# Norm ahead of the feed-forward stage: transposes and per-token statistics in place of averages over partitions, and the side work of the cycles dealt out anew

## What is computed

```python
def _layer(x, wqkv, qs, ksc, wo, lg, lb, w1, b1, w2, b2):
    q, k, v = split(shift_token(x) @ wqkv)        # 8 heads of 64
    q, k = rotary_xpos(l2norm(q) * qs, l2norm(k) * ksc)
    o = local_attention(q, k, v)                  # windows of 64, each looks one window back
    x = x + o @ wo
    h = shift_token(x)                            # features 64..127 come from the token before
    mu = h.mean(-1, keepdims=True)
    var = h.var(-1, keepdims=True)
    h = (h - mu) / jnp.sqrt(var + 1e-05) * lg + lb
    h = h @ w1 + b1
    a, g = jnp.split(h, 2, axis=-1)
    return x + (a * gelu(g)) @ w2 + b2
```

## Time and profile before

| | |
|---|---|
| device time, median of 3 runs | 1309.71 us (1308.45 to 1318.06) |
| the profiled execution, its own time | 1315.54 us |
| its span | 1313.7 us |
| busy share of the span | PE 96%, ACT 88%, POOL 87%, DVE 83% |
| mean granted TensorE clock | 0.994 |

### The profile page before, as it was taken

How to read it: one execution, slowest core, us unless ns; L and a number is a source line. 1 busy time by engine, 2 the same in 40 slices (tenths; PEclk the granted TensorE clock), 3 DMA queues, 4 the chain that set the end, 5 groups by cost and what they waited for, 6 DMA issues and landing times.

```text
span 1313.7 us, 38163 instructions
## 1 busy us (share of the span) xinstructions
PE 1264.7 (96%) x13793; PEld 1011.5 (77%) x13794; DVE 1088.4 (83%) x1883; ACT 1162.1 (88%) x3529; POOL 1147.3 (87%) x840
## 2 busy tenths in 40 slices
PE   7889999999999999899988999999999999999998
PEld 4777888888888887566657788888888888876776
DVE  6788888888888887599877888899988898983777
ACT  4778999999999998787768899999999999998886
POOL 4888999999999998399778999999999999984776
PEclk9999999999999999999998999999999999999999
DMA  5122222222222221011011222221112222110223
GB/s 165 35 74 62 62 62 66 66 62 62 62 70 70 58 50 38 17 32 38 1 29 30 46 46 46 50 50 46 46 46 47 51 52 50 38 39 25 66 79 97
DMA packets 60298, 70.04 MB, mean 53 GB/s; under 512 B 8912, under 2 KB 38288, under 8 KB 60112
## 3 DMA queue, kind: packets, MB, share of 16 engines
q1 hardware_dynamic: 60112, 67.61, 20.5%
HBM read 13.33 MB, written 4.19 MB: 13 GB/s over the span
## 4 chain that ended last, share of the span: by engine, by line
PE 75%; POOL 7%; ACT 6%; DVE 5%; issue 4%; DMA 2%; SPq 1%; ACTq 0%; DVEq 0%; POOLq 0%
PE ps L203 59%; PE ps L268 8%; PE ps L278 3%; PE ps L281 3%; POOL t L1259 3%; ACT P L655 3%; POOL hxr L1259 2%; DVE t L975 1%; POOL P L1259 1%; DMA norm<-X 1%; DVE nm L1006 1%; DVE t L987 1%; ACT sqk L629 1%; DVE sums L994 1%; POOL side L1289 1%
## 5 line engine op out<-in xcount | busy, mean ns | idle before, releaser
L655 ACT ACTIVATE P<-ps,nm 128x128 f32<-128x128 f32 x1024 | 364.2, 384 | 4.2 <-DVE nm L1006 4.1
L203 PE MATMUL ps<-wqkv,hT 128*128 128x512 f32 x1152 | 330.7, 429 | 14.4 <-DVE t L975 10.4
L1259 POOL TENSOR_TENSOR t<-t 128x1024 f32<-128x1024 f32 x128 | 307.5, 2402 | 32.8 <-DVE t L975 30.4
L1259 POOL TENSOR_TENSOR P<-P,rden 128x512 f32<-128x512 f32 x256 | 294.6, 1160 | 31.0 <-DVE rden L1013 28.9
L203 PEld LDWEIGHTS ps<-wqkv,hT 128*128 128x128 f32 x1152 | 217.0, 190 | 92.0 <-issue 28.4
L1259 POOL TENSOR_TENSOR t<-t,rr 128x1024 f32<-128x1024 f32 x128 | 244.0, 1906 | 19.7 <-ACT rr L638 19.3
L655 ACT ACTIVATION_READ_ACCUMULATOR P<-ps,nm 128x1 f32 x1024 | 230.1, 225 | 0.0
L987 DVE TENSOR_TENSOR t<-ps,tabl 128x512 f32<-128x512 f32 x256 | 164.1, 683 | 41.0 <-ACT sqk L629 39.3
L1259 POOL TENSOR_TENSOR hxr<-hxf,hxr 128x512 fp32r<-128x512 f32 (+1 forms) x93 | 130.8, 1434 | 67.9 <-ACT hxr L711 67.8
L1006 DVE TENSOR_REDUCE nm<-ps 128x4 f32<-128x512 f32 x256 | 173.4, 679 | 6.4 <-PE ps L203 6.3
L645 ACT ACTIVATE PT<-ps 128x1024 f32<-128x1024 f32 x128 | 130.5, 1019 | 48.2 <-PE ps L268 47.3
(11 more groups left out here) (140 smaller groups left out, 2548.5 us busy)
## 6 DMA issues: line engine op xcount, KB each, us to landing
Vs<-Vn SPq DMA_DIRECT2D x224, 128.0 KB, 2.3
side<-in_x SPq DMA_DIRECT2D x17, 256.0 KB, 2.9
A<-X SPq DMA_DIRECT2D x16, 256.0 KB, 2.5
...
```

The costliest lines, as they stand in the source:

```text
L203: return e.matmul(o, lhsT, rhs, start=start, stop=stop, skip_group_check=True)
L655: k = act(P[:, g, :], ps[:, 3 + s, (g % 4) * 128:(g % 4 + 1) * 128], ACT.Exp, bias=nm[:, g:g + 1], accum_out=den[:, g:g + 1])
L1259: return e.tensor_tensor(o, a, b_, op)
```

## The change

The averages over partitions go. The shifted block `h2` is turned by four transposes of 128x128 into PSUM with tokens on partitions (`turn_h`, kind 0), copied to SBUF by ACT (`keep_t`, kind 1), and DVE takes mean and variance of each token with the batch-norm instructions (`stats_h`, kind 2). ACT makes the root of four columns (`root_h`, kind 2), DVE subtracts and multiplies in place (`apply_h`, kind 3, four instructions of 128x128 with a column for mean and for factor), PE turns the block back (`turn_back`, next kind 0), and ACT copies it to where `scale_hc` had put it (`keep_h`, kind 0).

Dealt out anew: in layer 0 `ln_root` from kind 2 to 3, `ln_apply` from kind 3 to 0, `ln_turn` and `ln_keep` from kind 0 to 2, the shifts on POOL from kind 1 to 3; in layer 1 `rec_root` from kind 2 to 0, `rec_root2` from 1 to 3, `rec_input` from 2 to 0, `rec_scan` from 3 to 1, `shift_hi` from 0 to 2. The split of `w2` moves to the end of the attention part (from DVE to POOL), `set_decay` too. The waits for PSUM bank 2 stand in the steps themselves. In the feed-forward part of each layer the last block is done by the same new steps.

```diff
         norm = sb("norm", [128, 3 * L])
-        h2, sq, rsd = (norm[:, j * L:(j + 1) * L] for j in range(3))
+        h2, hn0 = (norm[:, j * L:(j + 1) * L] for j in range(2))
...
+        w1 = norm[:, 128:128 + 2 * HID]
+
+        w2 = norm[:, 1024:1408].rearrange("p (j d) -> p j d", j=3)
+        nst = norm[:, 1408:1432].rearrange("p (t k) -> p t k", t=TPB)
+        nmv = norm[:, 1432:1440].rearrange("p (t k) -> p t k", t=TPB)
+        nrs = norm[:, 1440:1444]
...
-            def mean(l, b, bank):
-                e.wait_ge(s_h2, 32 * (l * NB + b + 1))
-                mm(ps[:, bank, :], avg, h2[:]).then_inc(s_mu, 1)
-
-            def var(l, b, bank):
-                e.wait_ge(s_sqh, l * NB + b + 1)
-                mm(ps[:, bank, :], avg, rsd[:]).then_inc(s_va, 1)
+            def turn_h(l, b):
+                m, bank = l * NB + b, turn_bank(l, b)
+                e.wait_ge(s_h2, 32 * (m + 1))
+                if 0 < b < NB - 1:
+                    e.wait_ge(s_hn, m)
+                for t in range(TPB):
+                    k = e.transpose(ps[:, bank, t * 128:(t + 1) * 128], h2[:, t * 128:(t + 1) * 128], idf[:])
+                k.then_inc(s_nt, 1)
+
+            def turn_back(l, b):
+                m, bank = l * NB + b, back_bank(b)
+                e.wait_ge(s_na, m + 1)
+                if b < LATE:
+                    e.wait_ge(s_xadd, 2 * m + 4)
...
+                for t in range(TPB):
+                    k = e.transpose(ps[:, bank, t * 128:(t + 1) * 128], hn0[:, t * 128:(t + 1) * 128], idf[:])
+                k.then_inc(s_nu, 1)
...
+                    for b in due(i, 12, {LATE: NT + 3, NB - 1: -1}):
+                        turn_back(l, b)
                     if l and (b := hit(i, 6)) is not None:
...
-                    for b in due(i, -4, {0: -1, 1: -1, 2: TURN[2]}) if l == 0 else ():
...
                         e.wait_ge(s_x, b)
-                        side_free(l, i - 1)
+                        e.wait_ge(s_xadd, 2 * b - 3)
                         ln_turn(b, 2)
...
-                    if (b := hit(i, 8)) is not None:
-                        mean(l, b, 2)
-                    if (b := hit(i, 10)) is not None:
-                        var(l, b, 2)
+                        proj(l, b, 1)
+                    if (b := hit(i, 8)) is not None and b < NB - 1:
+                        turn_h(l, b)
...
+                e.wait_ge(s_nt, m + 1)
...
+                act(hn0, ps[:, turn_bank(l, b), :], ACT.Copy).then_inc(s_ht, 1)
+
+            def root_h(l, b):
                 m = l * NB + b
-                e.wait_ge(s_rv, m + 1)
-                act(rsd[:], rsd[:], ACT.Exp, scale=-0.5).then_inc(s_rs, 1)
-
...
+                e.wait_ge(s_ns, m + 1)
+                act(nrs, nmv[:, :, 1], ACT.Ln, bias=eps_ln).then_inc(s_nr0, 1)
+                e.wait_ge(s_nr0, m + 1)
+                act(nrs, nrs, ACT.Exp, scale=-0.5).then_inc(s_nr, 1)
...
+            def keep_h(l, b):
+                e.wait_ge(s_nu, l * NB + b + 1)
+                if l:
+                    e.wait_ge(s_hs, b + 1)
+                act(seq(B, b), ps[:, back_bank(b), :], ACT.Copy).then_inc(s_hn, 1)
...
-                    if (b := hit(i, 11)) is not None:
-                        log_var(l, b, 2)
+                    if (b := hit(i, 9)) is not None:
+                        keep_t(l, b)
+                    for b in due(i, 12, {LATE: NT + 3, NB - 1: -1}):
+                        keep_h(l, b)
...
+                    for b in due(i, 10, {LATE: NT + 2, NB - 1: -1}):
+                        root_h(l, b)
...
-                        for b in due(i, -4, {0: -1, 1: -1, 2: TURN[2]}):
+                        for b in due(i, -2, {0: -1, 1: -1, 2: TURN[2]}):
                             ln_keep(b, 2)
...
-                        for b in due(i, -6, {0: -1, 1: -1, 2: ROOT[2]}):
+                        for b in due(i, -5, {0: -1, 1: -1, 2: ROOT[2]}):
                             ln_root(b)
...
-                        if (b := hit(i, 12)) is not None:
-                            root_var(l, b)
-                        for b in due(i, 1, {0: 4, 1: 6}):
+                        for b in due(i, 3, {0: 4, 1: 6}):
                             rec_root2(b)
...
-                    if i == 6:
+                    if i == NT:
...
-                    if l == 0 and i == 9:
+                    if l == 0 and i == NT + 1:
...
+            def stats_h(l, b):
+                m, x = l * NB + b, hn0
+                e.wait_ge(s_ht, m + 1)
+                for t in range(TPB):
+                    k = e.bn_stats(nst[:, t, :], x[:, t * 128:(t + 1) * 128])
+                k.then_inc(s_nb, 1)
+                e.wait_ge(s_nb, m + 1)
+                for t in range(TPB):
+                    k = e.bn_aggr(nmv[:, t, :], nst[:, t, :])
+                k.then_inc(s_ns, 1)
+
+            def apply_h(l, b):
+                e.wait_ge(s_nr, l * NB + b + 1)
+                for t in range(TPB):
+                    x = hn0[:, t * 128:(t + 1) * 128]
+                    k = ts(x, x, nmv[:, t, 0:1], nrs[:, t:t + 1], ALU.subtract, ALU.mult)
+                k.then_inc(s_na, 1)
...
-                        if (b := hit(i, 13)) is not None:
-                            scale_hc(l, b)
-                        for b in due(i, -2, {0: -1, 1: 5}):
+                        for b in due(i, 0, {0: -1, 1: 5}):
                             rec_root(b)
...
+                    for b in due(i, 10, {LATE: NT + 1, NB - 1: -1}):
+                        stats_h(l, b)
+                    for b in due(i, 11, {LATE: NT + 2, NB - 1: -1}):
+                        apply_h(l, b)
                     if l == 0:
-                        if (b := hit(i, 12)) is not None:
-                            scale_hc(l, b)
                         for b in due(i, -7, {0: -1, 1: -1, 2: STATS[2]}):
                             ln_stats(b)
                     else:
                         if (b := hit(i, 8)) is not None:
                             rec_sum(b)
-                        if (b := hit(i, 9)) is not None:
-                            centre(l, b, 2)
                         if (b := hit(i, 6)) is not None:
                             rec_gamma(b, 2)
-                        for b in due(i, 3, {0: 5, 1: 8}):
+                        for b in due(i, 5, {0: 5, 1: 8}):
                             rec_scan(b)
...
-                    if l == 0 and 9 <= i < 12:
-                        set_decay(i - 9)
+                    if l == 0 and NT < i < NT + 4:
+                        set_decay(i - NT - 1)
...
-                    for b in due(i, 2, {0: 5, 1: 7}) if l else ():
+                    for b in due(i, 4, {0: 5, 1: 7}) if l else ():
...
-                        for b in due(i, -5, {0: -1, 1: -1, 2: NORM[2]}):
+                        for b in due(i, -4, {0: -1, 1: -1, 2: NORM[2]}):
                             ln_apply(b)
-                        for b in due(i, -3, {0: -1, 1: -1, 2: SHIFT[2]}):
+                        for b in due(i, -1, {0: -1, 1: -1, 2: SHIFT[2]}):
                             shift_hi(l, b)
                             shift_lo(l, b)
                     else:
-                        if (b := hit(i, -4)) is not None:
+                        for b in due(i, -2, {0: -1, 1: 0}):
                             shift_hi(l, b)
                         for b in due(i, -3, {0: -1, 1: 4}):
...
+                        e.wait_ge(s_w2hi, l + 1)
+                        tt(w2r[:, 1, :, :], w2, w2r[:, 0, :, :].bitcast(F32), ALU.subtract).then_inc(s_w2lo, 1)
```

More of the change, by code:

```diff
@@ L95, in program @@
         cw = [cols[:, 4 + j:5 + j] for j in range(4)]
-        one, eps_ln, eps_rms, ln2x8, mln2, part = (cst[:, i:i + 1] for i in range(6))
-        avg = part.to_broadcast([128, 128])
+        one, eps_ln, eps_rms, ln2x8, mln2 = (cst[:, i:i + 1] for i in range(5))
         ax, ez, u, dd, lnu, ru, half, nx, mx = (ab[:, i:i + 1] for i in range(9))
@@ L556, in tensor @@
                             e.wait_ge(s_ti, 2)
-                        var(l, NB - 1, 7)
+                        turn_back(l, NB - 1)
                     if l and 0 <= b - 2 < NB:
@@ L1228, in vector @@
                             if b == 1 and j == 0:
-                                centre(l, NB - 1, 7)
+                                stats_h(l, NB - 1)
+                            if b == 1 and j == 1:
+                                apply_h(l, NB - 1)
                         if l == 0 and b == NB - 1:
```

195 lines of the change are left out of this document (79 added, 116 removed).

## The result

After the change the kernel takes 1415.87 us (median of 4 runs, 1411.87 to 1417.73) where before takes 1311.49 (median of 4, 1308.45 to 1318.06): ratio 1.0795, 95% interval 1.0773 to 1.0818. The forecast was slower, 1326 us with a range to 1348; the change costs 104 us, not 15. The profiled execution after has a span of 1410.1 us, before 1313.7.

A forecast was written before the change was run, and what follows sets the result against it. PE's queue was taken as the bound, with ACT and POOL close to full. Four cycles +0.80 us in layer 0 and +0.76 in layer 1 gave 9.4 + 9.7 - 3 = +16 us, median 1326 us, range 1298 to 1348.

The forecast's parts named there:

- PE goes from step to step and its queue sets the time: Both layers before the change: no PE idle brackets, so PE's queue sets the intervals, 30.84 and 31.38 us for four cycles.
- the term -0.82 for each four cycles: PE, both layers: `mean` and `var` out, transposes in, 2 x (0.85 - 0.44) = 0.82 us gained per block.
- The sign set for it: Layer 0 after the change: interval 2 to 3 should be 6.3 to 6.8 us.
- has no room for an interval of 6.34 either: ACT in layer 1, 39.1 of 40 us busy: its lack counted as shorter than the stall of 1.13 us there.
- The cost of `apply_h`: DVE in layer 0, kind 3: collision with POOL's divisions costs up to 1.1 us or gains 0.42, taken as 0.2.
- the third rival: `apply_h` on DVE: each of four instructions waits out one POOL instruction, 73 us in all, about 1385 us; chance 0.05.
- `ln_apply` in kind 0: Layer 0, 0 to 1: POOL's 8.57 us meets PE's 6.78, 0.72 forgiven, a stall of 1.07 us in each four cycles.
- the forecast's sign: Layer 0: `turn_p` of kind 0 to kind 1 should be 7.7 to 8.2 us, PE waiting for POOL.
- `turn_back` waits for `proj_add`: Interval 3 to 0, both layers: PE waits for DVE to have read bank 2, 0.35 us with the semaphore.
- Layer 1, 2 to 3: `stats_h` ahead of `rotate` delays `add_qk` and the divisions: 7.47 us where PE could do 6.34, stall 1.13 us.
- The start: First cycles: taking the split of `w2` and `set_decay` out gives back at most 4.3 us, taken as 3.
- The scan in kind 1: Layer 1, 0 to 1: `rec_scan` adds 0.95 us to the divisions, costing 0 to 0.45 us, taken as 0.1.

The follow-up runs named there:

- b1: Kernel before, with the matmuls of `mean` and `var` cut to 8 columns and the `Ln` taken from SBUF: 1316.46 us, ratio 0.9995.
- e9: b1 with ACT's `keep_q` of the next tile moved ahead of the seventh exponential: 1345.97 us, ratio 1.0241.
- e11: Kernel before with only ACT's `keep_q` of the next tile moved ahead of the seventh exponential: 1343.82 us, ratio 1.0218.
- e7: e5 and e6 together on top of e1, subtraction and scaling still left out: 1313.45 us, ratio 0.9966 to before.
- e1: Changed kernel with `apply_h` cut to one column, so the norm's subtraction and scaling are left out: 1337.59 us.
- e2: Changed kernel with `apply_h` as one instruction of 512 columns in place of four of 128: 1341.40 us.
- e3: Changed kernel with an accumulator column added to the four `apply_h` instructions, values not the norm's: 1350.34 us.
- e8: e7 with the whole of `apply_h` put back as two DVE `tensor_tensor` instructions of 512 columns: 1457.98 us.
- e5: e1 with `ln_apply` put into kind 1 in place of kind 0: 1328.16 us.
- e6: e1 with `stats_h` and `apply_h` behind `rotate`, `turn_back` behind `turn_qk`, and `keep_h` and `root_h` moved to match: 1323.81 us.

## Why the prediction was right on the direction and wrong on the size

**"PE goes from step to step and its queue sets the time" failed**, and with it the term -0.82 for each four cycles. Measured: 0 to 0.14 (b1, e9 against e11). The sign set for it failed too: 2 to 3 in layer 0 was to be 6.3 to 6.8 and is 7.21. A timeline of PE without brackets shows that PE is never waiting, not that nothing else would wait if it were faster. The prediction saw ACT at 39.1 of 40 and said that it "has no room for an interval of 6.34 either", but took this for hidden behind other stalls and still booked the gain in intervals without one. The added transposes, though, did cost: in the long intervals, where PE is the limit, e7 has 8.42 for 8.01 and 8.44 for 8.05, 0.4 each, near the 0.44 that the earlier trace rows gave. So matmuls were taken from intervals where they were free and transposes put where they were not.

**The cost of `apply_h` failed**: 0.2 us for each four cycles of layer 0 and none in layer 1 were booked, where e1 shows 0.72 and 4.34. It was the third rival, given a chance of 0.05 and left outside the range. Its mechanism is what the rows at 888.28 to 890.50 and e1, e2 and e3 show: three of the four instructions in layer 1, and two in layer 0, wait out POOL's. It put the price at 3 us in all 24.4 periods and 1385 us; the mean over both layers is 2.6 us, and 1385 is still short of 1415.87 because the dealing comes on top. That the mean agrees is in part luck: layer 0 is far below 3 us, and layer 1 is above it by the lower clock too. What it was dismissed on, that 0.34 us for 128 columns is not shorter than the statistics, said nothing about waits beside POOL. The rule of the Trainium skill, SBUF — State Buffer, "Who interferes with whom", is that `tensor_scalar` can use both ports, and that of VectorE and GpSimd the one that comes second is then blocked until the other has finished, while the form with the accumulator does not contend. e3 agrees (396 ns against a median of 666 and up to 1939), and so does its rule on two SBUF inputs with e8 (2.74 us against 0.69).

**`ln_apply` in kind 0** was priced at 1.07 us of stall; e5 gives 0.61, of which 0.44 falls in 1 to 2, as the wait [0.28 <-POOL P] stands in the second half of kind 1's `turn_p`. So 0 to 1 itself is 7.35 and not the 7.7 to 8.2 of the forecast's sign. The excess comes from the first failed step: with the real 7.19 in place of 6.78 the same sum gives 8.57 - 0.72 - 7.19 = 0.66.

**`turn_back` waits for `proj_add`**, 0.35 forecast: right mechanism and nearly the size. With `apply_h` out of the way e1's timeline has idle times of 0.28 us at it, and e6 took 0.47 off the interval; the 0.72 of the kernel after holds part of `apply_h`'s delay, which DVE carries on to `proj_add`.

**Layer 1, 2 to 3**, statistics ahead of `rotate`: forecast 7.47 in place of 6.34, measured 8.08. The delay was right, its path was not: the prediction followed it through `add_qk` and the divisions, and missed that `qk_proj` of the next tile waits for the last part of `rotate`, the bracket of 1.52 at 884.78. This same wait carried the delay of `apply_h` to PE, 2.43 at 895.51. It is the step of the list "who waits for that" that was left out.

**The start** gave 7.1 us, forecast 3; part of it is the clock, whose mean from 20 to 80 us is 0.97 before and 1.00 after. **The scan in kind 1** cost nothing that shows: 0 to 1 in layer 1 is 7.18.

In the terms of the forecast, four cycles: layer 0 apply 0.72, dealing 32.34 - 31.22 = 1.12, transposes and rest 0.27, in all +2.11 (+0.80 forecast); layer 1 4.34, 0.42 and 0.85, in all +5.61 (+0.76 forecast). e7's new order costs 0.49 in 0 to 1 of layer 1, which is part of that 0.85.
